# Source keys turned once per batch and broadcast from DRAM, with 40 of 50 plain tiles read by one-hots

## What is computed

```python
h = jnp.maximum(_layernorm(x, axis=-1), 0.0)
x = x + segment_sum((h * node_vec1)[src], dst) * node_vec1_n2          # layer 0
h = jnp.maximum(_layernorm(x, axis=-1), 0.0)
x = x + (1.0 + eps[0]) * h + segment_sum(relu(h[src] + edge_attr), dst)  # layer 1
```

## Time and profile before

| what | value |
|---|---|
| time, median of 3 runs | 4802.91 us (4801.01 to 4810.65) |
| the profiled execution's own time | 4791.23 us |
| its span, first to last instruction | 4789.2 us |
| mean granted TensorE clock | 0.914 |
| busy: PE, DVE, ACT, POOL | 78%, 80%, 68%, 73% |
| layer 0's batches | from about 192 to 3050 us |

### The profile page before, as it was taken

How to read it: one execution, slowest core, us unless ns; L and a number is a source line. 1 busy time by engine, 2 the same in 40 slices (tenths; PEclk the granted TensorE clock), 3 DMA queues, 4 the chain that set the end, 5 groups by cost and what they waited for, 6 DMA issues and landing times.

```text
span 4789.2 us, 130194 instructions
## 1 busy us (share of the span) xinstructions
PE 3721.2 (78%) x43852; PEld 2888.9 (60%) x43852; DVE 3812.7 (80%) x11454; ACT 3261.3 (68%) x9090; POOL 3497.5 (73%) x3590
## 2 busy tenths in 40 slices
PE   0388888888888888888888899467767777777775
PEld 0266666666666666666666666356666666666664
DVE  9788888888888888888888886767777776777775
ACT  1377777777777777777777777456666766666664
POOL 6757777777777777777777777477777777777774
PEclk9999999999999999999999999778888888888887
DMA  6322222222222222222222221211212221211221
GB/s 111 63 51 54 57 54 54 54 56 54 54 54 56 54 53 54 56 54 53 54 56 54 53 54 44 72 39 54 57 43 54 57 57 54 58 49 48 57 57 26
DMA packets 439702, 262.77 MB, mean 55 GB/s; under 512 B 334660, under 2 KB 423732, under 8 KB 432632
## 3 DMA queue, kind: packets, MB, share of 16 engines
q1 hardware_dynamic: 322488, 187.55, 16.7%
q0 software_dynamic: 110816, 60.69, 6.7%
q10 hardware_dynamic: 5728, 5.82, 0.5%
HBM read 172.96 MB, written 80.85 MB: 53 GB/s over the span
## 4 chain that ended last, share of the span: by engine, by line
PE 32%; POOL 23%; DVE 19%; issue 13%; ACT 10%; DMA 2%; DVEq 1%; ACTq 0%; SPq 0%; POOLq 0%
POOL stage L759 22%; PE candidates L1247 18%; PE plain_ps L1259 7%; DVE arena L1753 7%; ACT message L987 5%; DVE arena L1729 4%; ACT centered L956 2%; PE sorted_agg L1187 2%; PE candidates L1157 1%; ACT arena L880 1%; POOL message L759 1%; PE key_rows L1230 1%; DMA stage<-in_edge_attr 1%; DVE counts L1475 1%; PE key_rows L1139 1%
## 5 line engine op out<-in xcount | busy, mean ns | idle before, releaser
L771 POOL DMA_INDIRECT records<-stage,place_i x1875 | 1879.0, 1002 | 696.2 <-issue 652.0
L759 POOL DMA_INDIRECT stage<-table,src_plain x1250 | 1246.9, 997 | 409.1 <-issue 377.3
L987 ACT ACTIVATE message<-candidates,member_is 128x96 bf16<-128x96 f32 x4560 | 1170.7, 377 | 429.4 <-PE candidates L1247 426.3
L1753 DVE TENSOR_SCALAR arena<-window_iota,dst_rel 128x224 bf16<-128x224 f16 (+1 forms) x4800 | 1091.2, 302 | 37.8
L880 ACT ACTIVATE arena<-key_rows 125x640 f16<-125x640 f16 x1000 | 653.2, 716 | 215.1 <-DVE arena L1729 83.2
L1187 PE MATMUL sorted_agg<-arena 128*96 128x224 bf16 (+1 forms) x5000 | 654.1, 285 | 161.0 <-DVE arena L1753 109.6
L1259 PE MATMUL plain_ps<-summed,message 128*96 128x224 bf16 x4560 | 609.2, 269 | 68.2 <-ACT message L987 68.2
L1187 PEld LDWEIGHTS sorted_agg<-arena 128*96 128x96 bf16 x5000 | 543.7, 137 | 186.1 <-issue 118.6
L1259 PEld LDWEIGHTS plain_ps<-summed,message 128*96 128x96 bf16 x4560 | 490.7, 128 | 269.6 <-ACT message L987 127.4
L1729 DVE TENSOR_SCALAR arena<-arena,row_key 125x1280 bf16<-125x1280 f16 x1000 | 554.7, 555 | 96.5 <-ACT arena L880 64.6
L1139 PE MATMUL key_rows<-ident,record 128*125 128x128 f16 x5000 | 425.8, 235 | 239.2 <-DMA record<-records 96.2
(11 more groups left out here) (228 smaller groups left out, 5139.0 us busy)
## 6 DMA issues: line engine op xcount, KB each, us to landing
record<-records SPq DMA_DIRECT2D x50, 1650.0 KB
stage<-in_edge_attr SPq DMA_DIRECT2D x125, 400.0 KB, 3.2
records<-pad SPq DMA_DIRECT2D x25, 1650.0 KB, 11.9
records<-stage,place_i POOLq DMA_INDIRECT x1875
stage<-table,src_plain POOLq DMA_INDIRECT x1250
message<-table,mid_src POOLq DMA_INDIRECT x288
xs<-in_x SPq DMA_DIRECT2D x8, 390.6 KB
table<-parts ACTq DMA_DIRECT2D x4, 585.9 KB
```

Of the source, the lines that this page charges most:

```text
L759: pool.indirect_dma_start(message[:, k, j, :] if l == 0 else rows[:, k, j, :], None, table0 if l == 0 else table1, bass.IndirectOffsetOnAx ...
L771: pool.indirect_dma_start(records, bass.IndirectOffsetOnAxis(ap=place_i[:, h, e:e + 1], axis=0), stage[:, h, e, :], None).then_inc(scatter ...
L987: last = nc.scalar.activation(direct_message[n % DB][:, m * WIDE:(m + 1) * WIDE], candidates[n % 2][:, m * WIDE:(m + 1) * WIDE], ACT.Copy, ...
L1753: last = nc.vector.tensor_scalar(dst_onehot(g, t), window_iota[:, 0:WA if tile == 0 else WT], dst_rel[:, h, tile:tile + 1], None, ALU.is_e ...
```

## The change

The source keys of layer 0 come another way. PE turns a whole batch's keys by one transpose of 128 x 100 (`turn_all`), ACT copies the 100 x 128 result once (`copy_turned`) to `keys_turned`, SP stores this to DRAM (`turned`), waits for it to land, and loads each group's row of 1280 keys from there with a broadcast to 125 partitions, 320 KB (312.5 KiB) each time, 10 a batch. They land in four rooms (`key_of`: two as before, two more in a free part of `centered`), four groups ahead of their use. SP issues all of a batch's key loads before `load_stage` and `fill`, which thereby wait until the one-hots of group 5 are made. `turn_all` and `copy_turned` of the next batch stand where its first `turn_keys` and `copy_keys` stood.

`SIDE` is 20 and not 19: 40 plain tiles are read by one-hots, and 10 are gathered. All 8 steps now have 5 tiles.

```diff
-    SIDE = 19
+    SIDE = 20
-    CUTS = (0, 5, 10, 15, 19)
+    CUTS = (0, 5, 10, 15, 20)
+    turned = nc.dram_tensor("turned", (BATCHES, TILES * P), F16, kind="Internal").ap()
+        keys_turned = sb("keys_turned", [TILES, P], F16)
+        KEY_ROOMS = 4
+        def key_of(l, g):
+            return more_rows[:, g % 2, :] if l == 0 and g % KEY_ROOMS >= 2 else key_row[:, g % 2, :]
@@ SP, step0
-                sp_at_least(key_rows_ready[0], 2 * GROUPS * b)
+                sp_at_least(key_rows_ready[0], b)
                 sp_at_least(dst_onehot_ready[0], GROUPS * b)
                 load_record(0, b, 0)
+                sp.wait_ge(key_rows_copied[0], b + 1)
+                sp.sem_inc(loads_begun, 1)
+                sp.dma_start(turned_t[bass.ds(b, 1), :, :].rearrange("o t e -> (o t) e"), keys_turned[:]).then_inc(keys_stored, 16)
+                sp.wait_ge(keys_stored, 16 * (b + 1))
+                for g in range(GROUPS):
+                    nth = GROUPS * b + g
+                    if g == 0:
+                        sp_at_least(src_onehot_ready[0], 2 * GROUPS * b)
+                    elif g >= KEY_ROOMS:
+                        sp_at_least(src_onehot_ready[0], 2 * (nth - KEY_ROOMS + 1))
+                    sp.dma_start(key_of(0, g), turned_g[bass.ds(nth, 1), :].to_broadcast([NP, GE])).then_inc(keys_loaded[g % KEY_ROOMS], 16)
                 if left >= 2:
                     load_stage(b + 2, h)
                     fill(b + 2, h)
@@ ACT (PE's lines change alike: turn_keys to turn_all)
+                def copy_turned(b):
+                    act.wait_ge(key_rows_ready[0], b + 1)
+                    at_least(act, keys_stored, 16 * b)
+                    nc.scalar.activation(keys_turned[:], key_rows[0][0:TILES, 0:P], ACT.Copy).then_inc(key_rows_copied[0], 1)
-                        if g + 3 < GROUPS:
-                            copy_keys(b, h, u, g + 3)
-                            if n in (DIRECTS - 3, DIRECTS - 2):
-                                copy_keys(*after(b, h, u), n - (DIRECTS - 3))
+                            if n == DIRECTS - 3:
+                                copy_turned(b + 1)
@@ PE
+                def turn_all(b):
+                    pe.wait_ge(record_loaded[0][0], 16 * (b + 1))
+                    at_least(pe, direct_copied_keys, SUBS * b)
+                    nc.tensor.transpose(key_rows[0][0:TILES, 0:P], record16[:, 0, :, 2 * F], ident16[:]).then_inc(key_rows_ready[0], 1)
@@ DVE, src_onehots
-                    dve.wait_ge(key_rows_copied[l], 2 * nth + 2)
+                    if l == 0:
+                        uses = len(range(g % KEY_ROOMS, GROUPS, KEY_ROOMS))
+                        dve.wait_ge(keys_loaded[g % KEY_ROOMS], 16 * (uses * b + g // KEY_ROOMS + 1))
```

More of the change, by code:

```diff
@@ L134, in gnn_two_layers @@
     table1_v = table1.rearrange("(p c) f -> p c f", c=C)
+    turned = nc.dram_tensor("turned", (BATCHES, TILES * P), F16, kind="Internal").ap()
+    turned_t = turned.rearrange("b (t e) -> b t e", t=TILES)
+    turned_g = turned.rearrange("b (g e) -> (b g) e", g=GROUPS)
     records = nc.dram_tensor("records", (BATCHES * SLOTS + 2 * SE * P, ROW), F32, kind="Internal").ap()
@@ L265, in gnn_two_layers @@
         plain_key = sb("plain_key", [P, PLAIN, J])
+        keys_turned = sb("keys_turned", [TILES, P], F16)
+        KEY_ROOMS = 4
+        more_rows = centered_room[0:NP, :].bitcast(F16)[:, 2 * C * F - 2 * GE:2 * C * F].rearrange("p (k e) -> p k e", k=2)
+        assert MID * WT <= 2 * C * F - 2 * GE
+        def key_of(l, g):
+            return more_rows[:, g % 2, :] if l == 0 and g % KEY_ROOMS >= 2 else key_row[:, g % 2, :]
         row_order = sb("row_order", [P, BATCHES, PJ])
@@ L401, in gnn_two_layers @@
         key_rows_copied = per_layer("key_rows_copied")
+        keys_stored = sem("keys_stored")
+        keys_loaded = [sem(f"keys_loaded_{k}") for k in range(KEY_ROOMS)]
         src_onehot_ready = per_layer("src_onehot_ready")
@@ L749, in gather_mid @@
             def gather_mid(h):
-                pool.sem_inc(gathers_begun, 1)
+                pool.sem_inc(scatters_begun, 1)
                 for j in range(MID):
@@ L992, in step0 @@
                     if is_first(b):
-                        copy_keys(b, h, u, 0)
-                        copy_keys(b, h, u, 1)
+                        copy_turned(b)
                         copy_candidates(b, h, u, 0)
                     def group(g):
-                        if g + 3 < GROUPS:
-                            copy_keys(b, h, u, g + 3)
                         if g >= 1 and g + 1 < GROUPS:
@@ L1093, in _ @@
                         with act.Fori(0, UNITS) as s:
-                            act.wait_ge(far_sum, s + 1)
+                            act.wait_ge(far_sum, 2 * s + 1)
                             nc.scalar.activation(message[:, 0, :, 0:F], attr[:, 0, :, :], ACT.Relu).then_inc(far_first, 1)
-                            act.wait_ge(far_left, s + 1)
-                            nc.scalar.activation(message[:, 0, :, F:2 * F], attr[:, 0, :, :], ACT.Copy).then_inc(far_second, 1)
+                            act.wait_ge(far_sum, 2 * s + 2)
+                            nc.scalar.activation(message[:, 0, :, F:2 * F], attr[:, 0, :, :], ACT.Copy).then_inc(far_first, 1)
             for k in range(CHUNKS):
@@ L1284, in step0 @@
                     if is_first(b):
-                        turn_keys(b, h, u, 0)
-                        turn_keys(b, h, u, 1)
+                        turn_all(b)
                         pick(b, h, u, 0)
                     def group(g):
-                        if g + 3 < GROUPS:
-                            turn_keys(b, h, u, g + 3)
                         if g in (7, 8) and not is_last(b):
@@ L1318, in step0 @@
                                 mid_products(b)
-                            if n in (DIRECTS - 3, DIRECTS - 2):
-                                turn_keys(*after(b, h, u), n - (DIRECTS - 3))
+                            if n == DIRECTS - 3:
+                                turn_all(b + 1)
                         pick(*after(b, h, u), 0)
```

20 lines of the change are left out of this document (11 added, 9 removed).

## The result

| | before | after |
|---|---|---|
| time, median of 4 runs each | 4801.96 us (4800.14 to 4810.65) | 4989.73 us (4982.45 to 4993.55) |
| the profiled execution, its span | 4791.23, 4789.2 us | 4982.45, 4980.6 us |
| mean granted TensorE clock | 0.914 | 0.896 |

The ratio is 1.0386 with a 95% interval of 1.0366 to 1.0405. The change makes the kernel 3.9% slower; 4960 us was forecast, with a range of 4885 to 5045, and the time lies in it.

A forecast was written before the change was run, and what follows sets the result against it. Layer 0's batch chain was the bound: DVE in group phases, PE in wide phases, plus the handover. 74 + 90 - 10 + 1 + 2.6 = +157 us on 4791.2 gives 4948, 4960 us for the runs' median; range 4885 to 5045.

The forecast's parts named there:

- the handover: Between batches, keys' copy, store and first load in series: 7.1 us against 3.3, +3.8 us a batch, +90 us.
- the group phase: Each batch's group phase: DVE's key waits gone, less new waits and clock loss; -0.4 us a batch, -10 us.
- the tiles: Wide phase, two more tiles on PE less ACT's relief: +3.1 us a batch, +74 us over 24 batches.
- the ends: Batch 0's keys wait for ACT, +1 us; last batch waits for more of POOL's gathers, +2.6 us; layer 1 unchanged.
- the first broadcast load: Handover's first key row from DRAM: about 2.2 us fixed plus 2.5 us data at 128 GB/s, taken as 4.6 us.
- the loop's top: Group phase: PE's stop on issue stays and delays DVE through PE's pick, +0.4 us a batch in the mean.
- All engines for the loads: Rival, chance 0.12: key broadcast loads run on all DMA engines, 62 us less than forecast, 4898 us.
- POOL setting the period: Rival, chance 0.05: POOL's chain sets the batch time, two gathers less take 62 us off, 4741 us.
- The clock: Rival, chance 0.09: PE's granted clock drops in group phases, +4 instead of +0.5 us a batch, 5044 us.
- Slow broadcast reads: Rival, chance 0.04: key loads beyond 3.3 us each cost 10 us a batch per microsecond; 5200 us at 4.3.
- Keys in time: Rival, chance 0.04: at the handover keys land before DVE needs them, store and load in 3 us; 4828 us.
- The wait on PE's pick in the even batches: Group phase sign: DVE's waits on ACT's key copies replaced by waits on PE's pick, about 2 to 3 us.

The follow-up runs named there:

- e2: Kernel before with only the tile count changed, 40 plain tiles by one-hots and 10 gathered, keys still turned piece by piece: 4863.3 us (1.0122).
- e4: Changed kernel with each key row read into 128 partitions instead of 125: 4898.9 us (1.0197).
- e10: e3 with key rows read into 128 partitions instead of 125, still 40 tiles by one-hots: 4830.4 us (1.0047).
- e8: e10 with 36 tiles by one-hots and 14 gathered, instead of 40 and 10: 4780.7 us (0.9952).
- e1: Changed kernel with 38 plain tiles by one-hots as before, so the keys' new path alone: 4904.8 us (1.0206).
- e3: Changed kernel with the key transpose and copy five tiles sooner, and SP's sorted-word store and load moved one batch later, behind the key loads: 4848.5 us (1.0085).
- e7: e10 with 38 tiles by one-hots, and SP's stage loads and fill issued ahead of the store of the keys: 4910.8 us (1.0229).

## Why the prediction was right

The direction, the mechanism and the main terms held, and the sum was 34 us short: the handover 23 and the group phase 13 too low, the tiles 3, and the ends 6 too high, which hid a part of it. With the pieces of the table above, in us over the program:

| term | forecast | measured |
|---|---|---|
| two more wide tiles | +74 | 24 x (77.02 - 73.82) = +77 |
| the handover | +90 | 24 x (7.96 - 3.27) = +113 |
| the group phase | -10 | 24 x (40.09 - 39.96) = +3 |
| batch 0's keys | +1 | 0 |
| the end of layer 0, and layer 1 | +2.6 | -2 |
| span | +157 | +191 |

**The tiles.** Right: +3.1 forecast, +3.2 measured, in e2 alone as well as together. The trace bears out both parts of the sum. In the mean of 19 batches the 18th tile is copied 37.8 us after the first pick, for 38.8 before: ACT's relief of 1.0. From there to the third tile from the last it is 39.3 us for 35.0, the two picks 2.10 us apart twice.

**The handover.** Right in kind, short in one term. The copy and the step to SP came at 0.4 us for 0.6, the store with its wait at 1.93 for 1.9. The term that was too small is the first broadcast load: 5.9 us to DVE's start where I had 4.6 (my two parts, 2.2 and 2.5, come to 4.7). The packets in the trace tell which part. In the mean of 23 handovers the first packet starts 0.9 us after the issue, the 125th of 2560 bytes ends 4.2 us later, and DVE starts 0.6 us after that. So all but the data is 1.5 us, less than my 2.2, and the data take 4.2 where I had 2.5. The rate that I took from the earlier trace rows, 128 GB/s, is that of the loads behind the first: the second row comes 2.67 us later. The first load itself mostly ran at 61 to 98 GB/s, as the view above shows. Each packet took 0.10 us as later, with gaps between the packets. Why is not shown; SP issues the next three loads within the first 1.6 us of it. With 128 partitions (e4) the same three times are 1.0, 1.7 and 0.9 us: what 16 engines save is data time.

The rule of the Trainium skill that I had weighed against this, in "DMA: Bandwidth & Descriptors", section "Anatomy of one DMA — SWDGE (gpsimd) path", is a fit for DMAs that GpSimd issues, and SP issues this one. Its 2.0 us plus bytes at 436 GB/s give, as an estimate, 2.7 us of the load: less than half of what the changed kernel shows, and a microsecond under e4, where all engines take part. The measurement decides. The rule on the same page of the Trainium skill by which the partition count chooses the number of engines agrees with both rows of DMA shares above.

**The group phase.** Wrong in sign. DVE has no wait for key copies any more, but not all of the 2.3 us a batch was won. The second row cost +1.5 and not +1.0. For the loop's top I had allowed +0.4 on PE's account. From the 2 to 3 us in every second batch that I had worked out, over 1 would have followed, and with the transposes gone the pick could start at 1366.03, so even these were too much. Measured, DVE waited for PE's pick only 3.4 us in all. What cost time was DVE's own loop's top, in batches 6, 10, 14 and 18:

```profile
1451.98 2.43 DVE L1760 TENSOR_SCALAR arena<-centered,row_key 125x1280 bf16<-125x1280 f16 x4 [5.09 <-issue]
```

21.4 us in four stops, 0.9 a batch in the mean. Before the change DVE's idle time at that place was 3.9, 4.47, 2.9 and 2.9 us in these batches, all of it put down to ACT's key copies. So 14.1 of the 48.7 us that I had counted as won stayed and grew by 7.3. With -2.3, +1.5 and +0.9 the sum is the +0.1 us a batch that G shows. I had looked at PE's stop behind it and not asked whether DVE had one of its own.

**The end.** +2.6 forecast. PE's wait of the earlier trace rows grew by as much, from 7.87 to 10.45 us, but from S to the end of the last plain products the last batch is less than 1 us longer, within what two executions differ by.

**The rivals.** All engines for the loads: refuted by the 0.3 in the slices, and what e4 makes of it, worth 91 us where the rival had 62. POOL setting the period: refuted at 40 tiles (e2, e10), but real at 36 (e8), where two gathers more are 2.6 us of POOL's time a batch and cost the kernel 2 us in all. The clock: 0.78 and 0.89 in the group windows where the earlier trace rows had 0.84 and 0.91. The 0.78 is under the 0.8 that I had named as this rival's sign, so the sign came, but not its price of 4 us a batch: G is 0.1 us longer and in e1 no longer than before, W in e1 is as before, and e3 and e10, with the same light group phase, have a shorter G. Slow broadcast reads: no for nine loads of ten, 2.6 us each, under DVE's 3.3 a group; the first of a batch, at 4.2, is slower, and only the handover pays for it. Keys in time: not here, but what e3 makes of it, at 4848 us where the rival had 4828 (its own terms add up to 4825).

**The signs.** The DMA wait on DVE came in every handover, at 3.4 to 5.5 us (18.7 into the last batch, where DVE has less to do). The wait on PE's pick in the even batches did not come (3 waits, 1.4 us at most).

## What to carry to other kernels

When work is moved from the engines to a trip through DRAM, move its start too: most of the engine time saved was off the critical path, the 8 us of latency (copy, store, wait, load) was on it, and starting five tiles earlier, with the sort's loads moved aside, won back 141 of 188 us. A transfer small in bytes can be as slow as what is queued ahead of it (9.7 us and not 1.9 in e7), so issue the short urgent one first, and try a partition count that brings in all engines, as 128 did here for 125. And count the moved work on every engine that is nearly full: at 38 tiles here PE's and GpSimd's loads meet; two more cost some 50 us, two fewer give nothing.

## What was not expected of the hardware

- A broadcast read of one 2560-byte DRAM row into 125 partitions took 5.9 us to its user when it was the first of four issued together, 4.2 us of it data at about 76 GB/s; those behind it took 2.6 us each. Into 128 partitions the first took 3.8 us, 1.7 of it data.
- Three partitions more (125 to 128), 2.4% more bytes, made the whole kernel 1.8% faster (4989.7 to 4898.9 us).
- At the top of its loop DVE stops for 3.9 to 5.7 us beside loads on 5 engines, and for 2.7 to 3.3 us beside the same loads on 16. In the kernel before, without these loads, it stood 2.9 to 4.5 us there.
